# Two latent attentions in a tuned eight-sublayer program: three program orders changed

## The reference, cut to what matters

```python
q = rmsnorm(hidden @ Wq_a) @ Wq_b            # per head: 128 plain + 64 rotated elements
kv = rmsnorm(hidden @ Wkv_a) @ Wkv_b         # k_pass, v
q_rot = apply_rope(q_rot, cos, sin)          # cosine product plus sine product
k_rot = apply_rope(hidden @ Wk_rope, cos, sin)
scores = einsum('bqhd,bkhd->bhqk', qf, kf) * scale     # causal mask
p = softmax(scores)
o = einsum('bhqk,bkhd->bqhd', p, v).reshape(b, t, h*d_v) @ Wo
x = x + o
x = x + ternary_linear(layernorm(x))         # interleaved with the attention's batches
```

## Time and profile before

| | us |
|---|---|
| median of 3 runs | 3569.63 |
| lowest and highest of them | 3565.03, 3569.97 |
| span of the profiled execution | 3572.4 |
| PE busy in it | 3322.9 (93%) |
| DVE busy | 2352.9 (66%) |
| ACT busy | 1912.1 (54%) |
| POOL busy | 817.2 (23%) |

### The profile page before, as it was taken

How to read it: one execution, slowest core, us unless ns; L and a number is a source line. 1 busy time by engine, 2 the same in 40 slices (tenths; PEclk the granted TensorE clock), 3 DMA queues, 4 the chain that set the end, 5 groups by cost and what they waited for, 6 DMA issues and landing times. The chain is left out here.

```text
span 3572.4 us, 88785 instructions
## 1 busy us (share of the span) xinstructions
PE 3322.9 (93%) x34858; PEld 2714.8 (76%) x34858; DVE 2352.9 (66%) x6069; ACT 1912.1 (54%) x4767; POOL 817.2 (23%) x828
## 2 busy tenths in 40 slices
PE   6999986999999999999999789999789999999999
PEld 5777765888888888888888667777667777777787
DVE  4666655778787878787877546666545666666654
ACT  3554544666666666666666435545445454544543
POOL 2232321222222222222222223233200111111100
PEclk9999998999999999999999989999989999999999
DMA  6000000000000000000000030000000000000000
GB/s 224 1 1 1 1 1 22 17 23 17 23 17 20 20 20 20 20 19 15 20 20 20 26 133 1 1 1 1 1 1 1 1 1 1 1 4 4 4 7 10
DMA packets 51330, 66.69 MB, mean 19 GB/s; under 512 B 4962, under 2 KB 40291, under 8 KB 49379
## 3 DMA queue, kind: packets, MB, share of 16 engines
q1 hardware_dynamic: 50914, 61.00, 5.4%
HBM read 58.43 MB, written 2.56 MB: 17 GB/s over the span
## 5 line engine op out<-in xcount | busy, mean ns | idle before, releaser
L1285 DVE SCALAR_TENSOR_TENSOR d_acc<-d_raw,d_taps,d_acc 128x255 f32<-128x255 f32 (+2 forms) x1152 | 642.8, 599 | 146.7 <-ACT d_raw L1275 133.1
L2358 ACT ACTIVATE s_probs<-bank,s_nmax 128x128 f32<-128x128 f32 (+1 forms) x768 | 249.4, 436 | 369.9 <-DVE s_nmax L2350 369.9
L1510 ACT COPY d_power<-bank 128x768 f32<-128x768 f32 x320 | 259.0, 810 | 217.1 <-PE bank L1503 217.1
L1273 ACT ACTIVATE d_acc<-bank,d_tap_bias,d_taps 128x256 f32<-128x256 f32 x384 | 196.0, 561 | 167.1 <-PE bank L1254 160.6
L2350 DVE TENSOR_REDUCE s_nmax<-bank 128x4 f32<-128x512 f32 x192 | 174.7, 952 | 96.9 <-PE bank L2340 96.7
L698 POOL TENSOR_TENSOR a_q<-a_rope 64x512 f32<-64x512 f32 x128 | 163.3, 1276 | 279.4 <-DVE a_rope L688 238.3
L2381 DVE COPY s_probsT<-bank 128x384 f32<-128x384 f32 x192 | 106.8, 556 | 167.2 <-PE bank L2367 163.4
L738 ACT ACTIVATE a_area<-bank,a_nmax 128x128 f32<-128x128 f32 x256 | 93.7, 366 | 175.9 <-DVE a_nmax L729 175.7
L688 DVE TENSOR_TENSOR a_rope<-bank,a_sinT 32x512 f32<-32x512 f32 x256 | 177.4, 693 | 5.7
L183 POOL TENSOR_TENSOR rstd<-var_eps,minus_half 128x2 f32<-128x2 f32 x64 | 46.0, 718 | 585.5 <-DVE var_eps L165 449.3
L765 ACT COPY a_area<-bank 128x512 f32<-128x512 f32 (+1 forms) x260 | 138.4, 580 | 73.4 <-PE bank L756 72.0
(11 more groups left out here) (275 smaller groups left out, 9000.0 us busy)
## 6 DMA issues: line engine op xcount, KB each, us to landing
d_alpha<-d_alpha_rows SPq DMA_DIRECT2D x64, 256.0 KB, 3.5
d_g_decay<-d_running_rows SPq DMA_DIRECT2D x32, 258.0 KB, 3.4
a_w_o<-in_a_w_o SPq DMA_DIRECT2D x2, 2048.0 KB, 16.6
a_area<-in_a_q_nope SPq DMA_DIRECT2D x2, 1536.0 KB, 8.2
x<-in_x SPq DMA_DIRECT2D x8, 256.0 KB, 16.2
d_wk<-in_d_wk SPq DMA_DIRECT2D x1, 2048.0 KB
d_wq<-in_d_wq SPq DMA_DIRECT2D x1, 2048.0 KB
d_wv<-in_d_wv SPq DMA_DIRECT2D x1, 2048.0 KB
```

Source lines behind the costliest of these rows:

```text
L1273: nc.scalar.activation(acc[:, r % 3, j], b_proj[:, j * T:(j + 1) * T], ACT.Identity, scale=taps[:, r // 2, h, 3:4], bias=tap_bias[:, r // ...
L1285: last = nc.vector.scalar_tensor_tensor(out=acc[:, r % 3, j, d:T], in0=raw[:, r % 2, j, 0:T - d], scalar=taps[:, r // 2, h, 3 - d:4 - d], ...
L1510: nc.scalar.copy(power[:], b_step[:, :, 0:3 * P]).then_inc(g.step_out, 1)
L2358: last = nc.scalar.activation(probs[:, s % 2, i, cols], heads[:, i, cols], ACT.Exp, bias=nmax[:, s % 2, t, i:i + 1])
```

## The change: three orders inside a turn

Nothing is computed otherwise; the same instructions are issued in another order on three engines.

```diff
@@ PE, turn n
                         scores_pe(pe, n, 1)
+                    if n + 2 < PAIRS_ALL:
+                        project_pe(pe, n + 2)
                     if 0 < n <= PAIRS_ALL:
                         pv_pe(pe, n - 1)
-                    if n + 2 < PAIRS_ALL:
-                        project_pe(pe, n + 2)
@@ DVE, turn n
-                    if n > 1:
-                        oT_dve(dve, n - 2)
                     if n < PAIRS_ALL:
                         max_dve(dve, n, 0)
                         max_dve(dve, n, 1)
+                    if n > 1:
+                        oT_dve(dve, n - 2)
+                    if n + 2 < PAIRS_ALL:
+                        rope_dve(dve, n + 2)
                     if it + 1 < NB:
                         if p == 0:
                             mla_stats_dve(dve, it + 1)
...
                     if n < PAIRS_ALL:
                         recip_dve(dve, n)
-                    if n + 2 < PAIRS_ALL:
-                        rope_dve(dve, n + 2)
@@ POOL, turn n
                     pool.wait_ge(*g.q_rope_ready(0, min(n + 2, PAIRS_ALL)))
+                    if n + 2 < PAIRS_ALL:
+                        rope_pool(pool, n + 2)
+                        pool.wait_ge(*g.q_rope_ready(0, n + 3))
                     if it + 1 < NB:
...
                     spread_pool(pool, n)
-                    if n + 2 < PAIRS_ALL:
-                        pool.wait_ge(*g.recip_spread(0, n + 1))
-                        rope_pool(pool, n + 2)
+                    pool.wait_ge(*g.recip_spread(0, n + 1))
```

## The result

The changed kernel takes 3652.8 us (median of 4 runs, 3647.2 to 3660.4) against 3569.8 us before (4 runs, 3565.0 to 3571.3). The ratio is 1.0232, 95% interval 1.0216 to 1.0248: 83 us slower.

The account below looks back on a forecast made before the run. PE, busy 93% of the span, was taken to bound the kernel through its waits and clock. -13.7 + 33.2 + 24 + 3 + 6 + 34 = +86.5 us on the median 3569.6 gave 3656 us, range 3604 to 3690.

Parts of the forecast that it names:

- p = 3 and 4: Attention turns where the projection now precedes the values' product: both PE waits go, 0.98 us in 14 batches, -13.7 us.
- p = 1: Turn with rotation ahead of normalization L175: PE newly waits 2.37 us (bounds 1.48 and 2.37) in 14 batches, +33.2 us.
- Rival 1: L175 does not meet POOL's sum, so waits are shorter and fewer clock falls come: 3602 us, chance 0.18.
- p = 5: Values' product waits 3.4 us instead of 1.68, POOL's preparation now standing behind its sum; 14 batches, +24 us.
- p = 6: Ternary layer's normalization meets POOL's sum, its transposes starting slightly later; 12 x 0.25 = +3 us.
- Ends: First and last turns of the calls: late maxima and uncovered waits of the values' product, +6 us, bounds 0 and 10.
- Clock: PE's granted clock falls to half behind long idle times: 20 falls more, +34 us, bounds +5 and +49.
- Rival 2: Waits as forecast, but the clock hardly reacts more, only p = 5's waits bringing falls: 3627 us, chance 0.17.
- Rival 3: Faster: the projection covers every PE wait, taking the clock falls at p = 6 along: about 3505 us, chance 0.05.

Follow-up runs that it names:

- experiment 4: On the changed kernel, POOL's rotation sum waits at turns p = 1 and p = 6 until both L175 instructions are done, nothing moved; 3630.0 us.
- experiment 3: On the changed kernel, POOL's key preparation and inverse, with DVE's instructions feeding them, go ahead of the rotation at turn p = 4; 3572.9 us.
- experiment 2: On the changed kernel, DVE's token normalization L175 goes back ahead of the rotation at turns p = 1 and p = 6; 3559.0 us.
- the fastest version: On the kernel before, PE's new order plus the ternary layer's normalization ahead of the reciprocal and rotation at turn p = 6; 3486.8 us.

## Why the prediction was right

It said 3656 us and the runs gave 3652.8; the ratio makes the change +83 us on 3569.8 where the sum had +86.5. Term by term:

- **p = 3 and 4** (-13.7): right; none of the 28 waits is left in the trace, and PE's order alone is faster.
- **p = 1** (+33.2): right in place, cause and size, 2.35 against 2.37 us. That L175 would be held by POOL's sum, the choice between two bounds, is shown by experiment 4: the pair goes from 1.69 to 0.73 us when the sum is moved away and nothing else. Rival 1 is out (its sum has the ends at +5 where the forecast has +6, so its 3602 should read 3603).
- **p = 5** (+24): right; 12 idle times of 3.34 or 3.35 us and two of 3.63. That POOL's order causes it is shown by experiment 3 (0.21 us) and by POOL's order alone (5.00 us), that the maxima are part of it by the scaling put first (2.29).
- **p = 6** (+3): 2.13 against 2.12 us of idle time; 3.27 us from L811 to L192 (235.65 to 238.92) against 3.14 before (216.80 to 219.94), in ten of the twelve turns. In the other two the sum came late and did not hold L175, and it is 2.32 us. Together about zero instead of 3.
- **Ends** (+6): four waits of 1.14 us in the last turns and about 1.7 us more at each call's first L192 (3.84 and 3.81 against 2.07) make 8 us, less two waits of call 0's last turns that went (0.77 and 1.10): 6 us, as forecast.
- **Clock** (+34): 31 us by the mean clock. The number of falls came out too, 30 stretches in the loops against 14 + 17 = 31 forecast: 12 of the 14 idle times at p = 5 have one and 18 of the 26 others, five of them twice as long as before. But the rule behind it, one fall for each idle time over 3 us and two in three at 2.1 to 2.6 us, does not hold in the other kernels: 7 of 14 at 3.35 us in experiment 2, and of those of 2.07 to 2.14 us 13 of 22 with the keys first and 19 of 22 with the scaling first, where those of 2.29 us gave 2 of 12. That the clock's term fitted so closely is in part luck. Rival 2's place (few falls) could have been met with nearly the same waits. Experiment 4 was wrong on that point by 30 us.

Rival 3 failed where it was to be decided: the normalization ended at S + 5.8. But its waits do go, and its gain does come, once the tokens and keys are not behind the rotations: 3487 us, somewhat more than its 3505.

What stays open: in which cases an idle time of 2 to 3.4 us brings the clock down. Length alone does not decide it, as the scaling put first shows; no run moved such a wait by itself with its length and the work around it held.

## What to carry to other kernels

Before a producer is put earlier on an engine, list what it is put ahead of and who waits for that: here each rotation gained 0.8 us that nobody needed (the fastest version keeps it behind the reciprocal). Against that, p = 1's tokens were normalized at S + 5.8 instead of S + 1.4, and the latents' normalization of p = 4 started at S + 8.4 instead of S + 5.0. A move that is very harmful alone (the maxima, +152 us) can cost little behind another (27 us), so parts are judged in the order in which they would be combined. And two engines' instructions that hardly overlapped before a reorder may meet after it; the trace of the old kernel shows the price at other lines of the same shape.

## What the runs showed of the hardware

- A pair of `TENSOR_SCALAR` 128x256 f32 with two scalars per partition took 1.69 us with a POOL `TENSOR_TENSOR` (1.31 us) started 0.22 us behind its first instruction, 0.73 us without. It ended 0.16 us after POOL. Where the sum started 0.42 us behind the first instruction, and so behind the second one's start, the pair took 0.71 us and the sum 1.42 instead of the 1.27 it takes alone.
- This agrees with the Trainium skill (SBUF — State Buffer, section "Who interferes with whom"), by which, of a VectorE instruction in a two-port mode and one of GpSimd, the second to issue blocks until the first is done. That L175 runs in such a mode no run shows directly.
- PE's idle times of one length did not give one number of half-clock stretches: 12 of 2.12 us gave 11, 12 of 2.17 to 2.43 us in another kernel gave 5; 14 of 3.35 to 3.63 us gave 12 in the changed kernel, 7 in experiment 2 and 14 in experiment 4. In one kernel (scaling first) 12 of 2.29 us gave 2 and 22 of 2.07 to 2.14 us gave 19.
- The 14 of 1.68 us gave none, and in the loops none of 1.12 to 1.26 us gave one in any run.
